# A fused decoder layer: three weight splits moved to GpSimd, and the last token tile finished alone

## The reference

```
logits = x @ router_w + router_b + load_balancer
rw, sel = top_k(logits, 2); rw = softmax(rw)
e0 = silu(x @ sw_w1) * (x @ sw_w3) @ sw_w2
e1 = gelu(sym @ me_c1w + me_c1b) @ me_c2w + me_c2b         # sym: three linear layers of x
h2 = layernorm(syn + attn)                                 # syn, attn: linear layers of x
h2 = layernorm(h2 + relu(h2 @ ce_f1w + ce_f1b) @ ce_f2w + ce_f2b)
e2 = h2 @ ce_gen_w + ce_gen_b
e3 = gelu(x @ ml_w1 + ml_b1) @ ml_w2 + ml_b2
out = sum of the two selected experts, weighted by rw
```

## Time and profile before

| | us |
|---|---|
| median of three runs | 1557.3 (1554.55 to 1558.42) |
| the profiled execution, its own time | 1558.77 |
| its span, first to last instruction | 1557.0 |
| busy: TensorE matmul / VectorE / ScalarE / GpSimd | 1507.5 / 1142.5 / 847.5 / 368.5 |

### The profile page before, as it was taken

How to read it: one execution, slowest core, us unless ns; L and a number is a source line. 1 busy time by engine, 2 the same in 40 slices (tenths; PEclk the granted TensorE clock), 3 DMA queues, 4 the chain that set the end, 5 groups by cost and what they waited for, 6 DMA issues and landing times.

```text
span 1557.0 us, 28838 instructions
## 1 busy us (share of the span) xinstructions
PE 1507.5 (97%) x11294; PEld 1067.9 (69%) x11294; DVE 1142.5 (73%) x2310; ACT 847.5 (54%) x1122; POOL 368.5 (24%) x400
## 2 busy tenths in 40 slices
PE   8999999898999999999999999999999999999998
PEld 4334333334566666666656898888989898888887
DVE  6445555558799999999967877777676767777675
ACT  5888889764688888888874331222222221222221
POOL 1000001123445666667453310000000000000000
PEclk9999999998899999999999999999999999999999
DMA  7656665455465675656652100000000000000000
GB/s 158 132 110 124 129 117 99 69 94 104 64 111 92 99 104 88 108 85 86 101 172 68 62 1 15 1 14 1 1 15 1 14 1 15 1 15 1 1 15 14
DMA packets 61576, 97.37 MB, mean 63 GB/s; under 512 B 12461, under 2 KB 29881, under 8 KB 61441
## 3 DMA queue, kind: packets, MB, share of 16 engines
q1 hardware_dynamic: 61312, 95.34, 33.1%
q10 hardware_dynamic: 128, 0.20, 0.0%
HBM read 26.29 MB, written 4.19 MB: 20 GB/s over the span
## 4 chain that ended last, share of the span: by engine, by line
PE 86%; DVE 8%; ACT 2%; issue 2%; SPq 2%; DMA 0%; POOL 0%; POOLq 0%; DVEq 0%; ACTq 0%
PE ps L109 81%; PE ps L1203 2%; SPq L119 2%; DVE NM L1423 1%; ACT PX L1366 1%; DVE EE L699 1%; ACT H L578 1%; PE ps L1165 1%; PE ps L1211 1%; DVE XC L2034 1%; PE ps L1842 0%; PE ps L1833 0%; DVE X L775 0%; PE ps L1135 0%; DVE X L624 0%
## 5 line engine op out<-in xcount | busy, mean ns | idle before, releaser
L1423 DVE TENSOR_REDUCE NM<-ps 128x4 f32<-128x1024 f32 x256 | 307.7, 1220 | 34.5 <-PE ps L109 32.9
L1366 ACT ACTIVATE PX<-ps 128x1024 f32<-128x1024 f32 x256 | 262.4, 1025 | 83.0 <-PE ps L109 81.7
L578 ACT ACTIVATE H<-ps,b1c 128x1024 f32<-128x1024 f32 x256 | 268.4, 1120 | 47.1 <-PE ps L109 45.5
L1994 ACT ACTIVATE GF<-ps,cols 128x512 f32<-128x512 f32 x128 | 88.2, 689 | 295.7 <-PE ps L109 295.5
L109 PE MATMUL ps<-XC,W_sw_w 128*128 128x512 f32 x768 | 185.7, 392 | 0.0
L2185 DVE CAST GH<-GF 128x512 fp32r<-128x512 f32 x192 | 82.1, 427 | 106.9 <-ACT GF L1994 101.8
L109 PEld LDWEIGHTS ps<-XC,W_sw_w 128*128 128x128 f32 x768 | 140.5, 188 | 27.9
L2293 POOL TENSOR_SCALAR RSc<-AGc 128x4 f32<-128x4 f32 x23 | 6.9, 301 | 599.5 <-DVE AGc L2080 599.5
L109 PE MATMUL ps<-PX,VT 128*32 128x256 f32 x2048 | 140.0, 392 | 0.1
L2187 DVE TENSOR_TENSOR GH<-GF,GH 128x512 fp32r<-128x512 f32 x192 | 133.2, 694 | 6.6
L109 PE MATMUL ps<-KT,QT 48*128 48x512 f32 x512 | 129.4, 502 | 2.0 <-DVE NM L1423 1.9
(11 more groups left out here) (238 smaller groups left out, 2560.0 us busy)
## 6 DMA issues: line engine op xcount, KB each, us to landing
KT<-KS SPq DMA_DIRECT2D x128, 192.0 KB, 4.7
ST<-QS SPq DMA_DIRECT2D x254, 96.0 KB, 2.8
QT<-XSb SPq DMA_DIRECT2D x128, 96.0 KB, 4.1
XT<-in_xT_dram SPq DMA_DIRECT2D x8, 512.0 KB, 4.5
raw_a<-in_x_dram SPq DMA_DIRECT2D x8, 512.0 KB, 4.3
CR<-in_ctxT_dram SPq DMA_DIRECT2D x8, 512.0 KB, 4.5
out_dram<-X SPq DMA_DIRECT2D x7, 512.0 KB, 3.0
R_sw_w<-in_sw_w_dram SPq DMA_DIRECT2D x6, 512.0 KB, 5.8
```

Source lines behind the costliest of these rows:

```text
L578: e.activation(H1[s % 8][:, :, :], PP[s % 3][:, :, :], ACT.Tanh, bias=b1c[:, half:half + 1], scale=1.0).then_inc(act_th, 1)
L1366: e.activation(PX[s % 3][:, :, :, :], PP[2][:, :, :].rearrange("p g (c q) -> p g c q", c=2), ACT.Exp, bias=0.0, scale=0.25).then_inc(act_e ...
L1423: e.tensor_reduce(NM[u % 2][:, qc, :, :, i], PP[qc][:, :, :].rearrange("p g (m k) -> p g m k", m=2), AX.X, ALU.max, negate=True).then_inc( ...
L1994: e.activation(g[:, :], o, f, bias=cols[:, col:col + 1], scale=1.0).then_inc(act_g, 1)
```

## The change

Three tiles (the second half of sw_w2, ce_f2w, me_c2w) leave the chunks 3, 6 and 8 of the first pair, where ScalarE copied and VectorE subtracted, and GpSimd does both at steps 267, 275 and 283. In the last pair's end there are three groups of tiles, (0, 1), (2) and (3). For tile 3 the accumulation in bank 5 is closed with chunk 19's contribution, and the last four chunks go to a bank of its own, bank 2. VectorE adds the closed part behind tile 2's aggregate, and the rest when TensorE is done with tile 3; statistics, root, centering and transfer are made for tile 2 and for tile 3 alone.

```diff
--- before.py
+++ after.py
@@ -1608,9 +1608,9 @@
 
 LOADS = {238: (("sw_w1", 0), ("sw_w3", 0)), 243: (("sw_w2", 0), ("sw_w1", 1)), 258: (("sw_w3", 1), ("sw_w2", 1)),
          259: (("ce_f1w", 0), ("ce_f2w", 0), ("me_c2w", 0)), 278: (("ml_w1", 0), ("ce_gen_w", 0)), 279: (("ml_w1", 1), ("ml_w2", 0), ("ml_w2", 1))}
-POOL_TAKES = {243: ("sw_w1", 0), 245: ("sw_w3", 0)}
+POOL_TAKES = {243: ("sw_w1", 0), 245: ("sw_w3", 0), 267: ("sw_w2", 1), 275: ("ce_f2w", 0), 283: ("me_c2w", 0)}
 DVE_TAKES = {250: ("sw_w2", 0), 255: ("sw_w1", 1)}
-CHUNK_TAKES = {1: ("sw_w3", 1), 3: ("sw_w2", 1), 5: ("ce_f1w", 0), 6: ("ce_f2w", 0), 8: ("me_c2w", 0), 9: ("ml_w1", 0), 11: ("ml_w1", 1),
+CHUNK_TAKES = {1: ("sw_w3", 1), 5: ("ce_f1w", 0), 9: ("ml_w1", 0), 11: ("ml_w1", 1),
                12: ("ml_w2", 0), 13: ("ml_w2", 1), 15: ("ce_gen_w", 0)}
 ORDER = [*DVE_TAKES.values(), *CHUNK_TAKES.values()]
 
@@ -1619,6 +1619,10 @@
 
 GEN_BANKS = (7, 6, 0, 1)
 LAG = 3
+
+LAST = ((0, 1), (2,), (3,))
+
+APART = 24 * NP - 4
 
 ADDS = 28
 FIRST_BIASES = {19: (1,), 21: (2, 3)}
@@ -1787,11 +1791,11 @@
             for j in range(NP - 1):
                 w.wait_ge(dve_ctr, out_stats(j) + 1)
                 dma(e, out_tm[:, 4 * j:4 * j + 4, :], X1[:, 4 * j:4 * j + 4, :], d_out)
-            for u in range(2):
-                t = 4 * NP - 4 + 2 * u
+            for u, tiles in enumerate(LAST):
+                t = 4 * NP - 4 + tiles[0]
                 w.wait_ge(dve_ctr, 3 * NP + u)
-                dma(e, out_tm[:, t:t + 2, :], X1[:, t:t + 2, :], d_out)
-            w.wait_ge(d_out, 16 * (NP + 1))
+                dma(e, out_tm[:, t:t + len(tiles), :], X1[:, t:t + len(tiles), :], d_out)
+            w.wait_ge(d_out, 16 * (NP - 1 + len(LAST)))
 
         return early, rest
 
@@ -1914,8 +1918,11 @@
                         w.wait_ge(dve_ff, 2 * j + u + 1)
                     else:
                         w.wait_ge(dve_add, ADDS * j + 2 * u + {"sw": -2, "ce": 2, "ml": second_added(j) + 2}[x])
-                t = mm3(e, o, g[:, 0, 128 * v:128 * v + 128], g[:, 1, 128 * v:128 * v + 128], wt[:, 0, hc % 4, :], wt[:, 1, hc % 4, :],
-                        hc == 0 and v % 2 == 0, hc == last)
+                begins, ends = hc == 0 and v % 2 == 0, hc == last or (n == APART - 1 and v == 3)
+                if done is pe_last and v == 3:
+                    w.wait_ge(act_g, 24 * NP - 1)
+                    o, begins = P[2][:, 0:256], n == APART
+                t = mm3(e, o, g[:, 0, 128 * v:128 * v + 128], g[:, 1, 128 * v:128 * v + 128], wt[:, 0, hc % 4, :], wt[:, 1, hc % 4, :], begins, ends)
             if done is pe_second or hc == last:
                 t.then_inc(done, 1)
 
@@ -1950,9 +1957,9 @@
                     synergy(j)
                 for i in range(0 if j else len(EARLY), 24):
                     work(j, i)
-            for u in range(2):
-                for n in range(24 * NP - 4, 24 * NP):
-                    second(n, (2 * u, 2 * u + 1), pe_last)
+            for tiles in LAST:
+                for n in range(APART, 24 * NP):
+                    second(n, tiles, pe_last)
 
         return early, rest
 
@@ -2250,25 +2257,30 @@
                 for i in range(0 if j else len(EARLY), 24):
                     work(j, i)
             x1 = X1[:, 4 * NP - 4:4 * NP, :]
-            for u in range(2):
+
+            def add_last(v, o):
+                e.scalar_tensor_tensor(out=x1[:, v, :], in0=o, scalar=PB[:, v, 3:4], in1=x1[:, v, :],
+                                       op0=ALU.mult, op1=ALU.add).then_inc(dve_add, 1)
+
+            for u, tiles in enumerate(LAST):
                 w.wait_ge(pe_last, u + 1)
-                w.wait_ge(dve_add, ADDS * NP - 4)
-                for v in (2 * u, 2 * u + 1):
-                    o = P[4 + u][:, 256 * (v % 2):256 * (v % 2) + 256]
-                    e.scalar_tensor_tensor(out=x1[:, v, :], in0=o, scalar=PB[:, v, 3:4], in1=x1[:, v, :],
-                                           op0=ALU.mult, op1=ALU.add).then_inc(dve_add, 1)
-                w.wait_ge(dve_add, ADDS * NP - 2 + 2 * u)
+                w.wait_ge(dve_add, ADDS * NP - 4 if u < 2 else ADDS * NP)
+                for v in tiles:
+                    add_last(v, P[2][:, 0:256] if v == 3 else P[4 + v // 2][:, 256 * (v % 2):256 * (v % 2) + 256])
+                w.wait_ge(dve_add, ADDS * NP + (-2, -1, 1)[u])
                 w.wait_ge(dve_ctr, 3 * NP - 1)
-                for v in (2 * u, 2 * u + 1):
+                for v in tiles:
                     t = e.bn_stats(BN[:, v, :], x1[:, v, :])
                 seq.done(t)
                 seq.wait()
-                for v in (2 * u, 2 * u + 1):
+                for v in tiles:
                     t = e.bn_aggr(AG[:, v, :], BN[:, v, :])
                 t.then_inc(dve_ag, 1)
-            for u in range(2):
+                if u == 1:
+                    add_last(3, P[5][:, 256:512])
+            for u, tiles in enumerate(LAST):
                 w.wait_ge(pool_rs, 3 * NP + u)
-                for v in (2 * u, 2 * u + 1):
+                for v in tiles:
                     t = e.tensor_scalar(x1[:, v, :], x1[:, v, :], AG[:, v, 0:1], RS[:, v:v + 1], ALU.subtract, ALU.mult)
                 t.then_inc(dve_ctr, 1)
 
@@ -2312,14 +2324,15 @@
             for j in range(NP):
                 for i in range(0 if j else len(EARLY), 24):
                     work(j, i)
-            for u in range(2):
+            for u, tiles in enumerate(LAST):
                 w.wait_ge(dve_ag, 3 * NP + u)
                 w.wait_ge(dve_ctr, 3 * NP - 1)
-                rs, ag = RS[:, 2 * u:2 * u + 2], AG[:, 2 * u:2 * u + 2, 1]
+                n = len(tiles)
+                rs, ag = RS[:, tiles[0]:tiles[0] + n], AG[:, tiles[0]:tiles[0] + n, 1]
                 one.wait()
                 one.done(e.tensor_scalar(rs, ag, EPS, None, ALU.add), pool_seq)
                 one.wait()
-                one.done(e.tensor_tensor(rs, rs, nhalf[:, 0:2], ALU.pow), pool_rs)
+                one.done(e.tensor_tensor(rs, rs, nhalf[:, 0:n], ALU.pow), pool_rs)
 
         return early, rest
```

## The result

The changed kernel takes 1560.3 us in the median of 20 executions (1553.98 to 1565.1) against 1556.46 for the kernel before (20, 1549.58 to 1560.48). The ratio is 1.003 with a 95% interval of 1.0019 to 1.0041, so 3.0 to 6.4 us slower. I had forecast 2.6 us faster, with a range that ends at 1558.1 us, and had given a kernel slower by more than 0.3% a chance of 0.04. The profiled execution took 1560.68 us with a span of 1558.8.

A forecast was written before the change was run, and what follows sets the result against it. TensorE bounds the kernel, with 86% of the span on it. Gains of 1.97 us before ON's transposes and 0.65 us in the tail sum to 2.6 us, taking the median from 1557.3 to 1554.7 us, range 1551.8 to 1558.1.

The forecast's parts named there:

- What holds the gap: TensorE's 2.47 us idle before ON's transposes at 869.92 us: VectorE's queue behind the sw_w2 split; 0.30 would remain.
- the rival of another holder: Same gap: TensorE's transposes may wait for a second party as late as NTl; 1556.4 us, chance 0.12.
- three engines meet: Argument for another holder of the gap: three engines meet there within 1 us (865.06, 866.68 and 867.45).
- What GpSimd takes from VectorE: In VectorE's run from 863 to 867.7 us: GpSimd's work beside it costs 0.2 us, bounds nothing to 1.7.
- The evidence against the lock: VectorE's cast of GH at 890.80 us, issued while GpSimd was working, took 0.43 us as always.
- The lock rival: Before ON's transposes: GpSimd instructions shut VectorE out for their whole length, TensorE 1.5 us later; 1558.1 us, chance 0.10.
- The two later tiles: ce_f2w and me_c2w, split after 869.92 us where TensorE never waits: moving their work to GpSimd gains nothing.
- The tail: After the last matmul, three groups of tiles instead of two: gain 0.65 us, between -0.2 and 1.5.

The follow-up runs named there:

- the moved tiles: Kernel before with nothing on GpSimd, sw_w2's second half split behind chunk 6 instead of 3, ce_f2w behind 7 instead of 6: ratio 0.9989 to before.
- sw_w2 alone: Kernel before with only the second half of sw_w2 given to GpSimd, ce_f2w and me_c2w left with ScalarE and VectorE: ratio 1.0001 to before.
- the tail-only one: Changed kernel with the three tiles back on ScalarE and VectorE, the three tail groups kept: 1554.66 against 1556.55 us for the kernel before.
- the fills: Kernel before with no split on GpSimd, sw_w2 and ce_f2w split later, and seven GpSimd memsets of RR at step 267: one execution, gap 0.60 us.

## Why the prediction was wrong

1. *What holds the gap* was right: VectorE's queue behind the sw_w2 split, and nothing else. With the split taken out the gap was 0.49 us (0.30 forecast); the rival of another holder falls. Its argument that three engines meet "within 1 us" was misread too: 865.06 to 867.45 us are 2.4.
2. *What GpSimd takes from VectorE* was the step that failed: "So one delay of 0.23 to 0.43 us for some ten instructions ... I take 0.2". It was 5.06 us before NTl; with the 0.49 that the moved tiles left, that is the gap of 5.56 to 0.01. I treated 593 ns for LS as a price per instruction. It was a wait for the end of GpSimd's instruction, which there had only 0.6 us left to run. The changed kernel repeats the pair: GpSimd's ON ends at 857.49 + 1.02 = 858.51 us, LS at 857.94 + 0.60 = 858.54. Comparing ends, not durations, would have shown it, and the price of a split is then up to 2.4 us per held instruction, outside my bounds of nothing to 1.7 us in all. The kernel before even had VectorE work beside a GpSimd split, in phase B, which I passed over because it is no work of a chunk:

```profile
806.46 0.57 DVE L1492 TENSOR_TENSOR FB<-FB,C 128x128 f32<-128x128 f32 x1
...
809.14 0.35 DVE L1492 TENSOR_TENSOR FB<-FB,C 128x128 f32<-128x128 f32 x1
```

```profile
805.85 1.04 POOL L2285 CAST W_sw_w<-R_sw_w 128x1024 fp32r<-128x1024 f32 x1
806.97 2.38 POOL L2287 TENSOR_TENSOR W_sw_w<-R_sw_w,W_sw_w 128x1024 fp32r<-128x1024 f32 x1
```

The same operation takes 0.57 and 0.35 us and each time ends 0.14 us behind GpSimd's (807.03 against 806.89, 809.49 against 809.35).
3. *The evidence against the lock* was a cast not held at 890.80 us. It stood beside the normalisation of X. That one (a tensor_scalar with a column of scalars, beside which VectorE lost 0.23 us at most) and the power of VR at 853.84 us (GE keeps 0.16 us beside it) didn't hold VectorE for their length; the copies and subtractions of a split do, and so did the product ON. I took one kind of GpSimd instruction for all. Why those two kinds don't hold it stays open.
4. *The lock rival's mechanism* happened, and in its very order (GH by the copy, LS by the subtraction). It was priced 1.5 us over the old gap, the trace shows 3.1: it let chunk 5's subtraction of GH run as soon as its cast was done, where in the trace it met GpSimd's subtraction for ce_f2w and lost 2.02 us.
5. *The clock* was missing from every case. Behind the gap the granted clock is 0.50 through most of chunk 6, which is worth 2.4 us.
6. *The two later tiles* were costed at nothing. They begin as soon as the queue is free, and the gap is 5.56 us with them against 3.41 with sw_w2 alone.
7. *The tail* was right: 0.65 forecast, 0.78 in the changed kernel, 0.73 in the tail-only one.

## What to carry to other kernels

Before work goes to GpSimd, look up what VectorE does beside it, and compare where a stretched VectorE instruction ends with where GpSimd's ends: if they coincide, the price is up to the length of GpSimd's instruction, so cut it in pieces or move it away from the stretch that TensorE waits for. A queue with nothing to wait for runs ahead of its step, so work for later is not work at a later time. And cost a gap on TensorE with what its clock does behind it: here up to 2.4 us on top of the gap.

## What the hardware showed that I had not expected

- GpSimd's float32 copies and subtractions of 1024 columns hold a VectorE subtraction with both inputs in SBUF, a cast, and even a 128x16 operation, until they end (up to 2.2 us lost at once). Products with one input in PSUM were never held (0.68 us throughout). The Trainium skill (SBUF — State Buffer, section Who interferes with whom) says of both what is seen here: a VectorE instruction with two SBUF inputs, or a cast or tensor_scalar in a two-port mode, and a GpSimd instruction that reads SBUF shut each other out, whoever issues first, and an instruction with one SBUF input outside those modes is left alone. It also says that GpSimd instructions that only write leave an instruction with two inputs alone; the fills agree (GH 0.69 us). It does not agree for GpSimd's power, which reads SBUF too: beside its 3.51 us at 853.84 VectorE's GE operations kept 0.16 us.
- One gap of 2.47 us, two outcomes: chunk 6 at 3.02 us, or at 4.44 in another execution of the same kernel (4.59 in the tail-only one, whose first pair is the same). It is a part of the scatter between executions; the start of chunk 5, 857.05 to 862.12 us in three profiles of one kernel, is a larger one.
- The longest gap, 7.32 us, was followed by fewer slow matmuls (4.15 us for the 12) than those of 5.3 to 5.6 us (5.0 to 5.5). Why was not tried.
